# Graph attention on one core: owners' one-hot rows from squared distances on TensorE with one ScalarE pass, and the picked scores added in PSUM

## The chip, the cores and the metric

One Trainium2 chip, one of its NeuronCores. The metric is the device time of one execution in microseconds (us); a kernel is run several times and the median counts. Engines are called TensorE (PE in the profile, its weight loads PEld), VectorE (DVE), ScalarE (ACT), GpSimd (POOL) and SyncE (SP, which here only issues transfers).

## What is computed

Four graph layers after one another over 3125 nodes of 256 features and 100000 edges sorted by destination; each layer is added to `x`. Layers 0 (two convolutions) and 3 share this attention, here for one convolution with 4 heads:

```python
h = (x @ W).reshape(-1, H, C)
alpha_s = jnp.einsum('nhc,hc->nh', h, a_src)
alpha_d = jnp.einsum('nhc,hc->nh', h, a_dst)
e = jax.nn.leaky_relu(alpha_s[src] + alpha_d[dst], NEG_SLOPE)
m = jax.ops.segment_max(e, dst, num_segments=N)
ex = jnp.exp(e - m[dst])
s = jax.ops.segment_sum(ex, dst, num_segments=N)
alpha = ex / (s[dst] + 1e-16)
out = jax.ops.segment_sum(h[src] * alpha[:, :, None], dst, num_segments=N)
```

`alpha_s[src]` is one half of an edge's score (it comes with the gathered row), `alpha_d[dst]` the other (it is picked from a small table of the owners, the nodes that the edges are summed into). Layer 1 is a dot product attention, layer 2 a message sum; both keep their code.

## The kernel before

`sort_by_source` makes a second order of the edges; `units("d")` and `units("s")` cut each order into units, 128 edges that all belong to one group of 128 nodes, and store the lists and masks of the units in HBM. Then, layer by layer, `renew` projects the nodes and `attend` (lines 1354 to 1842) walks the edges. `attend` runs three times (tags 0a, 0b and none, here called stages 0a, 0b and 3); `attend_dot` and `aggregate_edges` are the stages of layers 1 and 2. Transfers that sort edges by source are spread over the stages (`moving`).

A stage of `attend` is 51 turns of 16 units (`STEP`). The order on each engine is written out by hand in its `step(t, sums, scores, spreads)`, which is called once per turn: turn t sums the units of turn t-1 (`sums`), computes the scores of the units of turn t, and prepares the owners' halves of turn t+1 (`spreads`). The lists `V`, `A` and `M` name the marks of VectorE, ScalarE and TensorE in this order, and `v.at(name, t)`, `s.at`, `m.at` are the counts that others wait for.

- GpSimd (1505) gathers a turn's 16 units, one indirect transfer of 128 rows each, with a memset of a buffer `pause` after each, three turns of buffers (`BUFS`) ahead. The slots of a quad (4 units) come free after its matmuls (`mm3`, `mm7`, `mm11`, `mm15`).
- TensorE: the transpose `scores` of the picked halves (1703) with 6 filling matmuls behind it (`keep_busy`, 104), then `reduce(0)`, `reduce(1)`, `reduce(2)`, each 4 fp32 matmuls one-hot x rows (1680), then 16 small matmuls `spread` (1692) that pick the owners' values with the one-hot rows `hot_r`, then `back_turned` (1723 and 1724, the exponentials back to columns), `reduce(3)`, 8 filling matmuls, and `joined` (1735), which turns the picked owners' values of the next turn round and adds their three bf16 parts.
- ScalarE: `extras` (1770) and `one_hot` (1759, 1763) for the quads' one-hots, `exp` (1796), `hot_rows` (1780, 1782), `alphas` (1810), `parts` (1816), `picked` (1823), `own` and `selfs` (1835, 1837). `hot_rows` makes the owners' one-hot rows of 8 units in two passes over 128 x 1024: an Abs of row minus partition number, and a Relu of one minus that. Its input `rows_r` is the row of the edges' owners, broadcast by SP to all 128 partitions (1465, 256 KB each).
- VectorE: `rescale`, `rows0` (1572), then a chain: `y` (1592, picked half plus own half), `leaky`, `withself` or `weigh`, the scans of the segment maximum, `under`, `shrink`, then `rows1`, `add0` to `add3` (1566), `rows2`, `add4` to `add7`, `rows3`, `add8` to `add15`, and `factor`.

```python
eng.wait_ge(vec, v.at(f"add{u - 4}", t) if u >= 4 else v.at(f"add{u + 12}", a))
```

ties matmul u to the addition that frees its PSUM bank: `mm4` waits for `add0`, and `add0` stands behind the whole chain of the scores and `rows1` on VectorE.

## Time and profile before

| | us |
|---|---|
| median of 3 timed runs | 7402.62 |
| lowest, highest | 7401.24, 7405.5 |
| span of the profiled execution, first to last instruction | 8931.6 |
| stage 0a of `attend` in it, from 997 to 2490 | about 1490 |

Only the span is known of the profiled execution, no time of its own beside it; it is 1529 us (20.7%) longer than the median of the timed runs. The profile page gives busy times over the span; over the whole of it GpSimd is busy 65%, TensorE 61%, VectorE 56%, ScalarE 43%, and the mean granted TensorE clock is 0.745. Times in the rows are in us from the start of the span unless marked ns. A matmul's end is modelled.

### The profile page before, as it was taken

How to read it: one execution, taken by the hardware profiler on the slowest of the kernel's cores; microseconds unless marked ns; L12 is line 12 of the kernel's file. 1: busy time of each engine (PE TensorE's matmuls, PEld its weight loads, DVE VectorE, ACT ScalarE, POOL GpSimd, SP SyncE). 2: the span in 40 equal slices, each digit the busy share in tenths (PEclk: the TensorE clock that was granted, in tenths of full speed). 3: DMA queues.
4: the chain of work that ended last, by engine and by line, in shares of the span. 5: the costliest groups of instructions: out<-in, count | busy, mean ns of one | idle time of the engine just before them, and what ended most of it. 6: DMA issues, size and time to landing. Idle time of an engine off the chain costs nothing. (4 is left out here: it accounts for less than half of the span.)

```text
span 8931.6 us, 130458 instructions
## 1 busy us (share of the span) xinstructions
PE 5412.5 (61%) x23088; PEld 4000.6 (45%) x23089; DVE 4963.7 (56%) x11653; ACT 3871.5 (43%) x9075; POOL 5847.5 (65%) x8186
## 2 busy tenths in 40 slices
PE   6442365666535656664676666658888754666665
PEld 5431244444424444443455555435555533444443
DVE  6444355555545555554677777744444445555556
ACT  2220255455424554552244444335555533454444
POOL 0555677777747777775467666657777765777774
PEclk9555677777767777776788988868888866777777
DMA  4112233333313333331466666423333323333332
GB/s 143 49 49 52 75 95 95 95 96 95 86 44 97 96 95 95 96 97 33 127 176 178 177 176 175 129 64 99 100 101 100 101 53 101 99 99 99 98 98 74
DMA packets 580940, 894.72 MB, mean 100 GB/s; under 512 B 307359, under 2 KB 357708, under 8 KB 580448
## 3 DMA queue, kind: packets, MB, share of 16 engines
q0 software_dynamic: 245984, 649.30, 26.7%
q1 hardware_dynamic: 334448, 218.84, 8.9%
q10 hardware_dynamic: 416, 25.60, 0.9%
q8 instruction: 27, 0.44, 0.0%
q14 instruction: 65, 0.53, 0.0%
HBM read 859.36 MB, written 59.47 MB: 103 GB/s over the span
## 5 line engine op out<-in xcount | busy, mean ns | idle before, releaser
L2002 POOL DMA_INDIRECT ad_ring<-tab_qv,ad_idx x808 | 770.7, 954 | 506.4 <-issue 217.6
L1515 POOL DMA_INDIRECT at_ring_0a<-tab_s,at_idx_0a x808 | 774.3, 958 | 430.9 <-PE at_po_0a L1680 219.2
L2396 POOL DMA_INDIRECT ae_ring<-tab_a,ae_idx x808 | 777.9, 963 | 423.0 <-PE ae_po L2553 233.7
L1515 POOL DMA_INDIRECT at_ring_0b<-tab_s,at_idx_0b x808 | 772.8, 956 | 426.7 <-PE at_po_0b L1680 213.2
L1515 POOL DMA_INDIRECT at_ring<-tab_s,at_idx x808 | 780.1, 965 | 377.6 <-PE at_po L1680 183.0
L1680 PE MATMUL at_po_0a<-at_rows_0a,at_hot_0a 128*128 128x264 f32 x1616 | 625.6, 560 | 520.8 <-ACT at_hr_0a L1780 199.8
L1680 PE MATMUL at_po_0b<-at_rows_0b,at_hot_0b 128*128 128x264 f32 x1616 | 624.3, 559 | 512.2 <-ACT at_hr_0b L1780 201.7
L1680 PE MATMUL at_po<-at_rows,at_hot 128*128 128x260 f32 x1616 | 614.5, 553 | 444.5 <-DVE acc L1566 179.0
L1680 PEld LDWEIGHTS at_po_0a<-at_rows_0a,at_hot_0a 128*128 128x128 f32 x1616 | 439.3, 282 | 670.8 <-DVE acc L1566 262.0
L1680 PEld LDWEIGHTS at_po_0b<-at_rows_0b,at_hot_0b 128*128 128x128 f32 x1616 | 438.5, 282 | 662.4 <-DVE acc L1566 264.4
L1680 PEld LDWEIGHTS at_po<-at_rows,at_hot 128*128 128x128 f32 x1616 | 435.9, 280 | 586.2 <-DVE acc L1566 225.4
L2182 PE MATMUL ad_pk<-node_a,ad_hr 128*128 x1616 | 485.0, 452 | 337.6 <-issue 193.1
L2546 PE MATMUL ae_pM<-ae_we,ae_featT 64*128 64x256 f32 x1616 | 508.0, 465 | 171.3 <-issue 114.5
L1566 DVE TENSOR_TENSOR acc<-acc,at_po_0a 128x264 f32 x808 | 314.0, 422 | 483.9 <-PE at_po_0a L1680 215.1
L1566 DVE TENSOR_TENSOR acc<-acc,at_po_0b 128x264 f32 x808 | 312.9, 422 | 481.5 <-PE at_po_0b L1680 212.2
L566 POOL DMA_INDIRECT recs_s<-rnk_recs_now,rnk_pos_now x294 | 288.8, 982 | 409.9 <-DVE rnk_both L466 176.2
L2182 PEld LDWEIGHTS ad_pk<-node_a,ad_hr 128*128 128x128 f32 x1616 | 350.6, 226 | 452.2 <-issue 396.8
L1566 DVE TENSOR_TENSOR acc<-acc,at_po 128x260 f32 x808 | 307.1, 418 | 437.7 <-DMA recs_s<-rnk_recs_now,rnk_pos_now 178.8
L2553 PE MATMUL ae_po<-ae_msg,ae_hot 128*128 128x256 f32 x1616 | 464.8, 439 | 98.1 <-issue 60.9
L2506 DVE TENSOR_TENSOR ae_pre<-ae_ring,ae_pM 128x1024 f32<-128x1024 f32 x202 | 246.6, 1221 | 493.4 <-PE ae_pM L2546 187.7
L2546 PEld LDWEIGHTS ae_pM<-ae_we,ae_featT 64*128 64x128 f32 x1616 | 351.2, 229 | 314.6 <-issue 178.7
L2353 DVE TENSOR_TENSOR acc<-acc,ae_po 128x256 f32 x808 | 291.5, 416 | 297.9 <-PE ae_po L2553 218.8
(508 smaller groups left out, 14085.4 us busy)
## 6 DMA issues: line engine op xcount, KB each, us to landing
at_rr_0a<-relrow_d SPq DMA_DIRECT2D x102, 256.0 KB
at_rr_0b<-relrow_d SPq DMA_DIRECT2D x102, 256.0 KB
ad_rr<-relrow_d SPq DMA_DIRECT2D x102, 256.0 KB
at_rr<-relrow_s SPq DMA_DIRECT2D x102, 256.0 KB
ae_feat<-attr_pad SPq DMA_DIRECT2D x808, 32.0 KB
rnk_lrow<-lorow_f SPq DMA_DIRECT2D x98, 256.0 KB
attr_pad<-in_edge_attr_dram ACTq DMA_DIRECT2D x1, 25000.0 KB, 79.1
at_ring_0a<-tab_s,at_idx_0a POOLq DMA_INDIRECT x808
```

The source lines that it names most:

```text
L566: eng.indirect_dma_start(out=order["s"]["recs"], out_offset=bass.IndirectOffsetOnAxis(ap=pos_now[:, t.slot, k:k + 1], axis=0), in_=recs_no ...
L1515: eng.indirect_dma_start(out=ring[:, t.slot * STEP + u, :], out_offset=None, in_=table, in_offset=bass.IndirectOffsetOnAxis(ap=idx[:, t.sl ...
L1566: v.did(f"add{u}", eng.tensor_tensor(to, to, po[:, u % 4:u % 4 + 1, 0:W], ALU.add))
L1680: m.did(f"mm{u}", eng.matmul(po[:, u % 4, 0:W], hot[:, q % 2, j, :], rows[:, q % 2, j, :, :].rearrange("p h f -> p (h f)"), start=True, st ...
L2002: eng.indirect_dma_start(out=ring[:, t.slot * STEP + u, :], out_offset=None, in_=table, in_offset=bass.IndirectOffsetOnAxis(ap=idx[:, t.sl ...
L2182: mm = eng.matmul(pk[:, p % 2, (u % 2) * D:(u % 2 + 1) * D], hot_r[:, u // HALF, (u % HALF) * P:(u % HALF + 1) * P], k_tab[:, bass.ds(gs[u ...
L2353: own(eng.tensor_tensor(to, to, out_ps(q, j), ALU.add), False)
L2396: eng.indirect_dma_start(out=ring[:, k, :], out_offset=None, in_=table, in_offset=bass.IndirectOffsetOnAxis(ap=idx[:, k:k + 1], axis=0))\
L2506: own(eng.tensor_tensor(pre[:, q % 2, :, :].rearrange("p (a u) f -> p a (u f)", a=2), ring[:, q * QUAD:(q + 1) * QUAD, :].rearrange("p (a ...
L2546: mm = eng.matmul(pM[:, j // 2, (j % 2) * D:(j % 2 + 1) * D], featT[:, q % 2, j, :], We[:, :], start=True, stop=True)
L2553: mm = eng.matmul(po[:, (q % 2) * 2 + j // 2, (j % 2) * D:(j % 2 + 1) * D], hot[:, q % 2, j, :], msg[:, q % 2, j, :], start=True, stop=True)
```

## The change

- `units` computes three rows per unit, `near`: the owner number (255 for edges that are no unit's own), and its square in two bf16 parts. Six VectorE instructions over 128 x 896 and three stores are added per call.
- In `attend`, SP loads `near` (3 partitions x 1024, 6 KB) in place of the broadcast rows. TensorE multiplies it with a constant `owner_rows` (2j, -1, -1) in four matmuls of 512 columns, `far0` to `far3`, into `far_bank` and `pb_bank`, which gives 2jr - r*r; ScalarE adds 1 - j*j as a bias and takes Relu, which is 1 where j equals r and 0 elsewhere: `owners0` to `owners3`, 128 x 512 each, from PSUM.
- `scores`, its 6 filling matmuls and VectorE's `y` are gone. The picked halves are added by one more matmul in `joined`'s accumulation, which now also waits for `picked`.
- `far0`, `far1` stand at the start of TensorE's turn, `far2`, `far3` between `reduce(0)` and `reduce(1)`; `owners0` and `owners1` open ScalarE's turn, `owners2` and `owners3` stand ahead of `one_hot(2)`.

```diff
+                    own(eng.scalar_tensor_tensor(out=own_f[:, :, :], in0=rel[:, :, :], scalar=FAR, in1=ok[:, :, :],
+                                                 op0=ALU.subtract, op1=ALU.mult))
+                    own(eng.tensor_scalar(own_f[:, :, :], own_f[:, :, :], FAR, None, ALU.add))
+                    own(eng.tensor_copy(near[:, 0, :, :], own_f[:, :, :]))
+                    own(eng.tensor_tensor(square[:, :, :], own_f[:, :, :], own_f[:, :, :], ALU.mult))
+                    own(eng.tensor_copy(near[:, 1, :, :], square[:, :, :]))
+                    own(eng.tensor_tensor(near[:, 2, :, :], square[:, :, :], near[:, 1, :, :], ALU.subtract))
...
+                    eng.wait_ge(chain, marks["near"])
+                    for part in range(3):
+                        eng.dma_start(od["near"][part, :, :].rearrange("(c p) e -> p c e", p=P), near[:, part, :, :])\
+                            .then_inc(saved, 16)
...
                     def feed_rows(t, h):
-                        eng.dma_start(rows_r[:, h, :], od["relrow"][bass.ds(t.n * STEP + h * HALF, HALF), :]
-                                      .rearrange("(o t) e -> o (t e)", o=1).to_broadcast([P, HALF * P])).then_inc(rows_in[h], 16)
+                        eng.dma_start(near[0:3, h, :], od["near"][:, bass.ds(t.n * STEP + h * HALF, HALF), :]
+                                      .rearrange("k t e -> k (t e)")).then_inc(rows_in[h], 16)
...
+                    eng.memset(near[:, :, :], 0.0).then_inc(blank, 1)
...
                         if scores:
-                            eng.wait_ge(mat, m.at("scores", t))
                             eng.wait_ge(act, s.at("own", a))
-                            v.did("y", eng.tensor_tensor(logits[:, 1, :], scores_in, logits[:, 0, :], ALU.add))
-                            done("y", t)
...
+                        def distances(p):
+                            h = p // 2
+                            if p % 2 == 0:
+                                eng.wait_ge(rows_in[h], t.n * 16 + 32)
+                            if p >= 2:
+                                eng.wait_ge(act, s.at(f"owners{p - 2}", t))
+                            m.did(f"far{p}", eng.matmul(far[p % 2], owner_rows[:, :],
+                                                        near[:, h, (p % 2) * QUAD * P:(p % 2 + 1) * QUAD * P],
+                                                        start=True, stop=True))
...
-                            m.did("scores", eng.transpose(scores_in, picked[:, :, :].rearrange("p h u -> p (h u)"), ident[:, :]))
-                            keep_busy(eng, spare_b, 6)
...
+                        distances(0)
+                        distances(1)
                         reduce(0)
+                        distances(2)
+                        distances(3)
                         reduce(1)
                         reduce(2)
...
-                                keep_busy(eng, spare, 8)
+                                keep_busy(eng, far_bank, 6)
                             eng.wait_ge(act, s.at("parts", t))
...
+                            eng.wait_ge(act, s.at("picked", t))
+                            eng.sem_inc(told, 1)
+                            m.did("joined", eng.matmul(joined[0:R, :], picked[:, :, :].rearrange("p h u -> p (h u)"),
+                                                       ident[:, :], start=False, stop=True, skip_group_check=True))
...
-                            s.did(f"far_r{h}", eng.activation(hot_r[:, h, :], rows_r[:, h, :], ACT.Abs, bias=minus_col[:, :]))
-                            done(f"far_r{h}", t)
-                            s.did(f"hot_r{h}", eng.activation(hot_r[:, h, :], hot_r[:, h, :], ACT.Relu, bias=ones[:, 0:1],
-                                                              scale=-1.0))
+                            eng.wait_ge(mat, m.at(f"far{p}", t))
+                            s.did(f"owners{p}", eng.activation(hot_r[:, p * QUAD * P:(p + 1) * QUAD * P], far[p % 2],
+                                                               ACT.Relu, bias=owner_bias[:, :]))
```

TensorE at the seam of two turns of stage 0a (`at_ta`, `at_tt`, `at_pe`, `at_po` are PSUM tiles of the scores, `joined`, the exponentials and the sums), before:

```order
L1680 MATMUL at_po_0a<-at_rows_0a,at_hot_0a 128x264
L107 MATMUL at_ta_0a<-ident 128x384 x8
L1733 REGISTER_ALU
L1735 MATMUL at_tt_0a<-ident,at_parts_0a 128x128 x3
L1699 REGISTER_ALU
L1701 REGISTER_ALU
L1703 MATMUL at_ta_0a<-ident,at_picked_0a 64x128
L107 MATMUL at_pb_0a<-ident 128x128 x6
```

And in the change:

```order
L108 MATMUL at_far_0a<-ident 128x512 x6
L1759 REGISTER_ALU
L1761 MATMUL at_tt_0a<-ident,at_parts_0a 128x128 x3
L1763 REGISTER_ALU
L1765 MATMUL at_tt_0a<-ident,at_picked_0a 64x128
L1712 REGISTER_ALU
L1715 MATMUL at_far_0a<-at_near_0a,owner_rows 128x512
L1715 MATMUL at_pb_0a<-at_near_0a,owner_rows 128x512
L1699 ISA
L1700 ISA
L1701 REGISTER_ALU
L1702 MATMUL at_po_0a<-at_rows_0a,at_hot_0a 128x264
```

The picked scores moved from a transpose of their own into `joined`'s tile; the two first distance matmuls stand where the six filling ones stood.

ScalarE from the start of a turn of stage 0a to the exponentials (`at_hr` is `hot_r`, `at_rows` the rows with the weights), before:

```order
L1770 ACTIVATE at_rows_0a<-at_al_0a 128x16x2
L1756 ISA
L1759 ACTIVATE at_hot_0a<-iota_row,at_nrel_0a 128x128 x4
L1746 REGISTER_ALU
L1763 ACTIVATE at_hot_0a<-at_hot_0a,ones 128x512
L1770 ACTIVATE at_rows_0a<-at_al_0a 128x16x2
L1795 ISA
L1796 ACTIVATE at_exp_0a<-at_less_0a 64x257
L1777 ISA
L1779 REGISTER_ALU
L1780 ACTIVATE at_hr_0a<-at_rr_0a,minus_col 128x1024
L1746 REGISTER_ALU
```

And in the change:

```order
L1799 ACTIVATE at_rows_0a<-at_al_0a 128x16x2
L1807 REGISTER_ALU
L1808 ACTIVATE at_hr_0a<-at_far_0a,owner_bias 128x512
L1807 REGISTER_ALU
L1808 ACTIVATE at_hr_0a<-at_pb_0a,owner_bias 128x512
L1785 REGISTER_ALU
L1788 ACTIVATE at_hot_0a<-iota_row,at_nrel_0a 128x128 x4
L1775 REGISTER_ALU
L1792 ACTIVATE at_hot_0a<-at_hot_0a,ones 128x512
L1799 ACTIVATE at_rows_0a<-at_al_0a 128x16x2
L1828 ISA
L1829 ACTIVATE at_exp_0a<-at_less_0a 64x257
```

The passes for the owners moved from behind the exponentials to ahead of the one-hots of quad 2.

## Rows read from the trace of the kernel before

**Rows 1.** Stage 0a: stretch; busy PE, PEld, DVE, ACT, POOL; clock, DMA share, GB/s.
```profile
970.00:2480.00 1510.00, 894.51 (x3711) 648.75 (x3711) 820.86 (x2004) 736.37 (x1727) 1064.35 (x1644) 0.73 0.35 94
```

**Rows 2.** Timeline, one turn of stage 0a: start, length, engine, line, tiles [idle before].
```profile
1702.46 0.48 DVE L1629 TENSOR_TENSOR_SCAN at_max_0a<-at_masks_0a,at_end_0a,at_full_0a 64x128 f32<-64x128 f32 x1
...
1705.36 5.65 PE L1680 MATMUL at_po_0a<-at_rows_0a,at_hot_0a 128*128 128x264 f32 x16 [4.77 <-ACT at_hr_0a L1780]
...
1713.99 0.33 PE L1724 MATMUL at_pe_0a<-ident,at_exp_0a 64*128 64x4 f32 x2
...
1714.25 2.05 PE L1680 MATMUL at_po_0a<-at_rows_0a,at_hot_0a 128*128 128x264 f32 x8
...
1717.57 0.28 ACT L1810 ACTIVATE at_al_0a<-at_pe_0a 128x128 f32<-128x128 f32 x1 [6.13 <-PE at_po_0a L1680]
...
1719.20 0.43 DVE L1566 TENSOR_TENSOR acc<-acc,at_po_0a 128x264 f32 x1 [6.81 <-DMA recs_s<-rnk_recs_now,rnk_pos_now]
...
1722.12 0.27 ACT L1835 ACTIVATE at_log_0a<-at_tt_0a 64x128 f32<-64x128 f32 x1 [1.78 <-DMA recs_s<-rnk_recs_now,rnk_pos_now]
...
1722.59 0.24 ACT L1770 ACTIVATE at_rows_0a<-at_al_0a 128x32 f32<-128x32 f32 x1
...
1723.99 1.21 DVE L1572 TENSOR_TENSOR at_rows_0a<-at_ring_0a,at_pe_0a 128x1024 f32<-128x1024 f32 x1
...
1725.43 3.88 PE L1680 MATMUL at_po_0a<-at_rows_0a,at_hot_0a 128*128 128x264 f32 x8 [5.78 <-DVE at_rows_0a L1572]
...
1727.15 0.28 DVE L1592 TENSOR_TENSOR at_log_0a<-at_ta_0a,at_log_0a 64x128 f32<-64x128 f32 x1 [1.95 <-PE at_po_0a L1680]
...
1731.17 0.48 DVE L1629 TENSOR_TENSOR_SCAN at_max_0a<-at_masks_0a,at_end_0a,at_full_0a 64x128 f32<-64x128 f32 x1
...
1731.29 0.24 ACT L1770 ACTIVATE at_rows_0a<-at_al_0a 128x32 f32<-128x32 f32 x1
...
1734.07 6.64 PE L1680 MATMUL at_po_0a<-at_rows_0a,at_hot_0a 128*128 128x264 f32 x16 [4.76 <-ACT at_hr_0a L1780]
```

**Rows 3.** Groups of instructions with forms, 1200 to 2300 us: count, busy us, mean ns, idle before.
```profile
L1515 POOL DMA_INDIRECT at_ring_0a<-tab_s,at_idx_0a x612 | 586.3, 958 | 315.3 <-PE at_po_0a L1680 184.1 <-issue 73.7 <-DMA recs_s<-rnk_recs_now,rnk_pos_now 36.4
...
L1519 POOL MEMSET at_pause_0a<- 128x256 f32 x611 | 199.7, 327 | 0.3
...
L1763 ACT ACTIVATE at_hot_0a<-at_hot_0a,ones 128x512 f32<-128x512 f32 x154 | 111.2, 722 | 5.0
L1782 ACT ACTIVATE at_hr_0a<-at_hr_0a,ones 128x1024 bf16<-128x1024 bf16 x76 | 87.2, 1148 | 2.5
L1780 ACT ACTIVATE at_hr_0a<-at_rr_0a,minus_col 128x1024 bf16<-128x1024 bf16 x76 | 86.1, 1133 | 0.0
...
L1816 ACT ACTIVATE at_parts_0a<-at_pb_0a 128x384 f32<-128x384 f32 x38 | 18.4, 485 | 0.0
...
L1823 ACT ACTIVATE at_picked_0a<-at_ring_0a 128x64 f32<-128x64 f32 x38 | 12.0, 316 | 0.0
...
L1703 PE MATMUL at_ta_0a<-ident,at_picked_0a 128*64 128x128 f32 x39 | 11.4, 292 | 0.0
...
L1592 DVE TENSOR_TENSOR at_log_0a<-at_ta_0a,at_log_0a 64x128 f32<-64x128 f32 x38 | 10.7, 283 | 85.2 <-PE at_po_0a L1680 62.5 <-ACT at_log_0a L1835 14.7 <-ACT at_rows_0a L1770 8.0
```

**Rows 4.** The addition `y` in stage 0a: count, min/median/max ns, first and last start.
```profile
L1592 DVE TENSOR_TENSOR at_log_0a<-at_ta_0a,at_log_0a x51: 282/283/284, 1024.3 to 2490.3; 64x128 f32<-64x128 f32 x51
```

**Rows 5.** Timeline of `units("s")`, VectorE and SP.
```profile
7424.58 0.63 DVE L729 CAST un_relb_s<-un_rel_s 128x896 bf16<-128x896 f32 x1
7425.23 0.40 SPq L824 DMA_DIRECT2D relrow_s<-un_relb_s  x1
...
7425.90 1.09 DVE L733 SCALAR_TENSOR_TENSOR un_ok_s<-un_rel_s,un_ok_s 128x896 f32<-128x896 f32 x1
```

**Rows 6.** Busy time by stretch, as Rows 1: under `reduce(3)` and under `reduce(0)`.
```profile
1714.20:1716.30 2.10, 2.10 (x11) 1.67 (x11) 0.00 (x0) 0.00 (x0) 1.80 (x3) 1.00 0.40 99
1725.40:1729.30 3.90, 3.87 (x8) 2.52 (x8) 1.75 (x7) 0.00 (x0) 2.61 (x5) 0.50 0.37 101
```

More of the change, by code:

```diff
@@ L1376, in attend @@
                 "add8", "add9", "add10", "add11", "add12", "add13", "add14", "add15", "factor"])
-        A = (["ext0", "away1", "hot1", "ext1", "away2", "hot2", "ext2", "exp", "far_r0", "hot_r0", "far_r1", "hot_r1",
+        A = (["owners0", "owners1", "ext0", "away1", "hot1", "ext1", "owners2", "owners3", "away2", "hot2", "ext2", "exp",
               "away3", "hot3", "ext3", "alphas", "parts", "picked", "away0", "hot0", "own"] + (["selfs"] if own_max else []))
-        M = ["scores", "mm0", "mm1", "mm2", "mm3", "mm4", "mm5", "mm6", "mm7", "mm8", "mm9", "mm10", "mm11",
-             "spread0", "spread1", "back_turned", "mm12", "mm13", "mm14", "mm15", "joined"]
+        M = ["far0", "far1", "mm0", "mm1", "mm2", "mm3", "far2", "far3", "mm4", "mm5", "mm6", "mm7", "mm8", "mm9", "mm10", "mm11",
+             "spread", "back_turned", "mm12", "mm13", "mm14", "mm15", "joined"]
         with ExitStack() as c:
@@ L1682, in reduce @@
                                                            start=True, stop=True))
[L1684 removed]
+                        def distances(p):
                             if not spreads:
[L1686 to L1691 removed]
+                                return m.skip(f"far{p}")
+                            h = p // 2
[6 more added lines that the diff above has]
+                                                        start=True, stop=True))
@@ L1692, in spread @@
+                        def spread(gs):
+                            if not spreads:
+                                return m.skip("spread")
+                            eng.wait_ge(act, s.at("owners3", t))
+                            for u in range(STEP):
                                 mm = eng.matmul(pb[:, u, :, :].rearrange("p k c -> p (k c)"),
-                                                hot_r[:, h, k * P:(k + 1) * P],
+                                                hot_r[:, u * P:(u + 1) * P],
@@ L1814, in step @@
                         if spreads:
-                            eng.wait_ge(mat, m.at("spread1", t))
+                            eng.wait_ge(mat, m.at("spread", t))
+                            if scores:
+                                eng.wait_ge(mat, m.at("joined", a))
                             s.did("parts", eng.activation(parts[:, :, :, :],
@@ L1836, in step @@
                             if own_max:
-                                s.did("selfs", eng.activation(logits[:, 2, :], joined[R:2 * R, :], ACT.Copy))
+                                s.did("selfs", eng.activation(logits[:, 1, :], joined[R:2 * R, :], ACT.Copy))
                         else:
```

94 lines of the change are left out of this document (45 added, 49 removed).

## The prediction

> **What bounds the kernel now.** I read the busy times of stage 0a first [rows 1]: in 1510 us GpSimd is busy 1064, TensorE 895, VectorE 821, ScalarE 736. No engine is full, so what sets a turn is either a chain of waits across engines or the pace of GpSimd. Then I read one turn in the timeline [rows 2]. The same scan starts at 1702.46 and 1731.17, so a turn is 28.7 us; three stages have 51 each, 153 turns.
>
> The chain goes round like this [rows 2]. VectorE multiplies the first rows at 1723.99 (1.21 us), then `y` starts at 1727.15 after 1.95 us of idle time, which is not a wait for data: 15 register loads (`groups`) stand between, and the two things that `y` waits for, the transpose and `own` (1722.12 plus 0.27), are long there. From `y` through the scans, `rows1` and `add0` VectorE needs 6.9 us until TensorE can start the eight matmul pairs of quads 1 and 2 at 1734.07. It has stood idle 4.8 us there, and `add0` is what it waits for in the code. Those sixteen instructions take 5.65 or 6.64 us, then come `spread`, `back_turned`, `reduce(3)`, the last additions, `factor`, `rescale` and the first rows of the next turn. So each instruction of VectorE between `y` and `add0` is on the ring; ScalarE's owner passes, SP's transfers and TensorE's `scores` are not, each ends before something later is due.
>
> GpSimd is the other limit: a gather takes 0.958 us, the memset behind it 0.327 [rows 3], and with the 0.16 us between them sixteen need 16 x 1.44 = 23.0 us. In the profile that leaves 5.7 us of each turn idle.
>
> The profiled execution spans 8931.6 us, the timed runs have a median of 7402.6, a factor of 0.829. The rows show one place where that time may lie: `back_turned` is issued at 1713.99 and ends by the model at 1714.3, but `alphas`, which waits for it alone, starts at 1717.57; the matmuls of `reduce(3)` are issued from 1714.25 on, but the first addition of one starts at 1719.20 [rows 2]. TensorE's marks arrive 3 to 5 us late there. If all stages shrink alike, a timed turn is 28.7 x 0.829 = 23.8 us, which is 0.8 us above GpSimd's 23.0. That nearness is the largest doubt of this prediction. Sums below are in us of the profiled execution and are carried over to the median unscaled, since instruction durations should be the same in both.
>
> **The change, part by part.**
>
> *VectorE's chain.* `y` goes: 283 ns [rows 4] and its own completion wait, 0.03 us between neighbours. 0.31 us per turn on the ring, x 153 = **-48 us**.
>
> *ScalarE.* Per turn 2 x (1.133 + 1.148) = 4.56 us of passes over 128 x 1024 go [rows 3]. Four Relus over 128 x 512 from PSUM come. The trace has none; bounds are the copy of 128 x 384 from PSUM at 0.485 us and the Relu of 128 x 512 from SBUF at 0.722 us [rows 3]. I take 0.65, being nearer to the size of the second: 2.6 us. ScalarE is relieved of 2.0 us per turn (1.7 to 2.6) at no gain, for its passes stood after `exp` and ahead of `one_hot(3)`, which waits for `mm7` anyway. What counts is where the new ones stand. `owners0` and `owners1` (1.3 us) now precede `extras(0)`, which ended at 1722.83, while the rows that `reduce(0)` also needs end at 1725.20: 2.4 us of cover. `owners2` and `owners3` wait for `far2` and `far3`, so `one_hot(2)` and `extras(2)` (ending at 1731.53) come later by 1.3 us and by the two matmuls; quad 2 is needed about 2.8 us behind 1734.07, so 5 us of cover. `exp` is pushed by about 1.2 us, and its reader `back_turned` comes 9 us later. If these covers went, the price is in the rivals.
>
> The Trainium skill, page "ScalarE: Activation LUTs", section "What ACT_TABLE_LOAD costs", gives about 280 ns plus 0.833 ns per element for an activation with a bias pointer, 707 ns for 512 columns as an estimate. That would be 2.8 us for the four, and since they lie off the ring the sum is the same.
>
> *TensorE.* Out: the transpose (0.29 us) and fillers of 6 x 128 columns. In: two distance matmuls of 512 columns in their place, about the same work, and two more between `reduce(0)` and `reduce(1)`, where it stood idle for 4.8 us [rows 2]; 1024 columns are 0.4 us at 2.4 GHz and 0.9 at 1.2. Zero on the ring. Fillers ahead of `joined` keep their 3072 columns. `joined` waits for `picked` too, which ScalarE does right behind `parts` (0.32 us), and has one fp32 matmul more (0.29 us, [rows 3]): up to 0.6 us later. `leaky` takes `own` at about 1727, 4.8 us after it is there, so this costs nothing while that holds.
>
> *SP and the DMA engines.* As many transfers per turn, 6 KB in place of 256 KB each. They are loaded two turns ahead and a matmul frees them earlier than the Relu did, so no queue waits longer. The DMA engines are 0.35 busy in the stage [rows 1]; taking 0.5 MB per turn from them frees nothing that is waited for. `feed_idx` waits for the previous `joined` in place of `scores`, issued back to back before.
>
> *`units`, twice.* Six VectorE instructions over 128 x 896 on its chain: three like the cast or scaling (0.63) and three with two inputs (1.09) [rows 5], 5.2 us, plus 6 x 0.03, about 5.4 us. After them come the evacuations that the stage's end waits for, so all of it shows: 2 x 5.4 = 10.8. The three stores add 3 x 0.40 us of issue on SP, in `units("s")` at its end, and some transfer time: 2 us, between 0 and 5. In `units("d")` they lie under the second list. **+13 us**.
>
> *Starts.* The memset of `near` is short of the 16 first gathers that the stage waits for, and the five tiny setup instructions run while VectorE waits for the inputs. Zero.
>
> Sum: -48 + 13 = **-35 us**, 8931.6 to 8897 in the profile and 7402.6 to **7368** in the timed runs. A measurement of this kernel can tell about 0.2%, 15 us, from no change.
>
> **The rivals.**
>
> *A, the forecast: the ring loses one instruction.* For it: of the 85.2 us that VectorE idles ahead of `y` in 38 turns only 14.7 are put down to `own` [rows 3]; the rest is the register loads. 7368.
>
> *B, GpSimd sets the timed turns.* If 23.0 us of gathers already decide there, a shorter chain only lengthens idle time elsewhere. For it: 23.8 against 23.0. Against it: GpSimd idles 5.7 us per turn in the profile. The change then also "does nothing" although it works. -0 + 13 = 7416, still within 0.2%.
>
> *C, `own` becomes the last to arrive (slower).* With TensorE's marks 3 to 5 us earlier in the timed runs, VectorE reaches `leaky` sooner, while `joined` still stands behind eight or six fillers and now also behind `picked` and a fourth product: +0.32 + 0.29, less the 0.31 of `y`, +0.3 us per turn, 46 us, with `units` 59: 7462. It decides from the point where `own`'s 4.8 us of cover fall under 0.6. For it: the turns in which `own` was already the releaser [rows 3]. ScalarE's new order would act at the same place with up to 1.3 us. Against it: the profile's cover.
>
> *D, TensorE's clock.* Under `reduce(3)` the granted clock is 1.00, which is 2.4 GHz, and eight instructions take 2.05 us; under `reduce(0)`, after TensorE has stood idle 5.8 us, it is 0.50, 1.2 GHz, and eight take 3.88 [rows 2, 6]. The sixteen of quads 1 and 2, after another idle 4.8 us, take 5.65 to 6.64 where 2 x 2.05 = 4.1 would do. `far2` and `far3` now lie in that gap. If they keep the clock up, a turn loses 1.5 to 2.5 us in the profile; in the timed runs GpSimd's 23.0 would stop it at 0.8 us per turn, -116, with `units` -103: 7300. Against it: 0.9 us of work in a gap of 4.8 is little.
>
> The Trainium skill, page "TensorE: Matmul & The Clock Gate", section "What's actually happening", says that half rate is the default and recent activity releases it; by that rule the filled gap speaks for D, and the trace agrees in that both slow stretches follow idle ones.
>
> **How the numbers follow.** A 0.42, B 0.26, C 0.22, D 0.10. Point 7368 from A. A's own range by the bounds (stores 0 to 5, 0.28 to 0.33 us per turn) is 7362 to 7375. The range reaches down to 7280, which takes in D, and up to 7460, the middle of C. Faster by over 0.2%: D and nearly all of A, 0.50. Within: most of B and the rest of A, 0.25. Slower: C and the part of B in which `units` costs over 15 us, 0.25.
>
> **What would show it.** Right: 153 turns of 28.4 us, `leaky` straight behind the register loads, four Relus of 0.59 to 0.72 us, VectorE busy about 33 us less in all (43 us of `y` less, 10 more in `units`). Against A: a turn unchanged in the profile with more idle time before `leaky` put down to `own` (C), more GpSimd share near 16 x 1.44 (B), or a granted clock well above 0.73 in the stages (D). The prediction is wrong if the time leaves the range, or if it moves in a stage other than these three and `units`.

## The result and the profile after

The changed kernel takes **7361.46 us** (median of 4 runs, 7357.06 to 7367.2), the kernel before in the same comparison 7404.06 (7401.24 to 7406.44): ratio 0.9943, 95% interval 0.9929 to 0.9957, 42.6 us faster. The forecast was 7368.

The profiled execution of before that the rows ahead come from was 20.7% longer than its timed runs; that of the changed kernel (span 7362.5) is as long as its own. The two can't be subtracted. So the kernel before was profiled again, unchanged (run e1_before below), with a span of 7395.2. "Before" means this second profile from here on, and the rows ahead are named by group.

From the two pages, engines' busy times and the queues of SyncE (q1) and of the instructions (q14), first before:

```profile
span 7395.2 us, 130458 instructions
PE 5003.2 (68%) x23088; PEld 3761.1 (51%) x23089; DVE 5017.3 (68%) x11653; ACT 3881.1 (52%) x9075; POOL 5854.0 (79%) x8186
...
q1 hardware_dynamic: 334448, 218.84, 10.9%
...
q14 instruction: 65, 0.53, 0.0%
```

and after:

```profile
span 7362.5 us, 129092 instructions
PE 5126.0 (70%) x22635; PEld 3674.3 (50%) x22636; DVE 4959.3 (67%) x11520; ACT 3550.9 (48%) x9075; POOL 5855.8 (80%) x8186
...
q1 hardware_dynamic: 297692, 141.87, 7.7%
...
q14 instruction: 140, 1.15, 0.0%
```

A queue's row gives its packets, the MB that they moved and their share of time. ScalarE is relieved of 330 us (2.2 us a turn), SyncE's queue moves 77 MB less, and the instruction queue moves 75 packets more, for which nothing in the change accounts.

Where the time went is read from one instruction that comes once a turn. `own` stands 51 times in each stage; the columns are its shortest, middle and longest duration in ns and its first and last start in us. Before:

```profile
L1835 ACT ACTIVATE at_log_0a<-at_tt_0a x51: 253/271/273, 847.4 to 2035.8; 64x128 f32<-64x128 f32 x51
L1835 ACT ACTIVATE at_log_0b<-at_tt_0b x51: 253/271/272, 2189.4 to 3378.1; 64x128 f32<-64x128 f32 x51
L1835 ACT ACTIVATE at_log<-at_tt x51: 253/255/273, 6165.7 to 7327.6; 64x128 f32<-64x128 f32 x51
```

After:

```profile
L1866 ACT ACTIVATE at_log_0a<-at_tt_0a x51: 252/253/270, 852.9 to 2004.4; 64x128 f32<-64x128 f32 x51
L1866 ACT ACTIVATE at_log_0b<-at_tt_0b x51: 252/253/270, 2163.9 to 3317.5; 64x128 f32<-64x128 f32 x51
L1866 ACT ACTIVATE at_log<-at_tt x51: 252/270/272, 6116.2 to 7295.3; 64x128 f32<-64x128 f32 x51
```

Fifty turns of 0a fall from 1188.4 us to 1151.5 (a turn from 23.77 to 23.03), those of 0b from 1188.7 to 1153.6 (23.77 to 23.07), and stage 3 **rises** from 1161.9 to 1179.1 (23.24 to 23.58). That is -36.9, -35.1, +17.2. Most of the rest is `units` (below). So there are three things to explain: why 0a and 0b gain more than twice the forecast 16 us each, why they stop at 23.0, and why stage 3 loses.

GpSimd's groups answer the second (why 23.0). Columns as in [rows 3]; first before, then after:

```profile
L1515 POOL DMA_INDIRECT at_ring<-tab_s,at_idx x808 | 780.5, 966 | 162.3 <-issue 98.7
L1515 POOL DMA_INDIRECT at_ring_0a<-tab_s,at_idx_0a x808 | 774.8, 959 | 159.6 <-issue 109.1
```

```profile
L1539 POOL DMA_INDIRECT at_ring<-tab_s,at_idx x808 | 782.6, 969 | 176.5 <-issue 97.3
...
L1539 POOL DMA_INDIRECT at_ring_0a<-tab_s,at_idx_0a x808 | 773.3, 957 | 139.1 <-issue 107.5
```

A gather costs the same as in [rows 3]. Its idle time in 0a falls to 139 us over 808 gathers, nearly all of it the 0.16 us from one instruction to the next: GpSimd has no free time left, and 16 x 1.44 = 23.0 us is the turn. Stage 3, whose gathers take 0.966 us, was at GpSimd's pace (23.2) before the change already. ScalarE's `picked`, which reads the gathered rows, shows the same from the other side: in 0a it waited for a gather in 9 of 51 turns before and in 50 of 51 after, in stage 3 in 42 of 51 before the change already.

TensorE's timeline of 0a changes too. Before, a turn from its `reduce(3)` (the first row of 128x264):

```profile
1508.47 2.05 PE L1680 MATMUL at_po_0a<-at_rows_0a,at_hot_0a 128*128 128x264 f32 x8
1510.35 1.46 PE L107 MATMUL at_ta_0a<-ident 128*128 128x384 bf16 x8
1511.65 0.83 PE L1735 MATMUL at_tt_0a<-ident,at_parts_0a 128*128 128x128 f32 x6
...
1514.15 2.04 PE L1680 MATMUL at_po_0a<-at_rows_0a,at_hot_0a 128*128 128x264 f32 x8 [1.23 <-DVE at_rows_0a L1572]
1522.86 6.50 PE L1680 MATMUL at_po_0a<-at_rows_0a,at_hot_0a 128*128 128x264 f32 x16 [6.66 <-ACT at_hr_0a L1780]
```

and after:

```profile
1499.40 0.40 PE L1765 MATMUL at_tt_0a<-ident,at_picked_0a 128*64 128x128 f32 x2 [1.21 <-ACT at_picked_0a L1854]
...
1503.20 3.60 PE L1702 MATMUL at_po_0a<-at_rows_0a,at_hot_0a 128*128 128x264 f32 x8 [2.63 <-ACT at_rows_0a L1799]
1506.63 0.38 PE L1715 MATMUL at_far_0a<-at_near_0a,owner_rows 128*128 128x512 bf16 x1
1506.85 0.38 PE L1715 MATMUL at_pb_0a<-at_near_0a,owner_rows 128*128 128x512 bf16 x1
1508.11 2.05 PE L1702 MATMUL at_po_0a<-at_rows_0a,at_hot_0a 128*128 128x264 f32 x8 [0.89 <-DVE acc L1591]
1510.60 2.05 PE L1702 MATMUL at_po_0a<-at_rows_0a,at_hot_0a 128*128 128x264 f32 x8 [0.44 <-ACT at_rows_0a L1799]
1513.08 2.10 PE L1724 MATMUL at_pb_0a<-b_tab,at_hr_0a 128*128 x16 [0.43 <-ACT at_rows_0a L1799]
```

Before, `reduce(0)` runs early and at full rate (2.04 us; its four fp32 matmuls stand as eight instructions, x8), TensorE then stands idle for 6.66 us until `add0` (the row names a ScalarE pass, but `mm4` waits for `add0` in the code), and the sixteen instructions of quads 1 and 2, which are on the ring, take 6.50. After, the same `reduce(0)` comes late and takes 3.60, off the ring, under VectorE's scans: between 2.04 and the 3.88 of [rows 2], which is half rate [rows 6]; the sixteen run at 2.05 us per eight and are through in 4.6. The granted clock says the same. The columns are those of [rows 1]; first before, `reduce(0)` and the first 4 us of the sixteen, then after, `reduce(0)` and quads 1 and 2:

```profile
1514.15:1516.19 2.04, 2.04 (x8) 1.43 (x8) 0.24 (x1) 1.20 (x4) 1.72 (x4) 1.00 0.41 95
1522.86:1527.00 4.14, 4.14 (x10) 3.21 (x11) 3.24 (x7) 3.55 (x4) 3.65 (x7) 0.50 0.54 144
```

```profile
1503.20:1506.80 3.60, 3.60 (x9) 2.69 (x10) 3.33 (x13) 1.89 (x6) 3.23 (x5) 0.56 0.39 101
1508.11:1512.65 4.54, 4.09 (x16) 2.87 (x16) 4.54 (x10) 4.47 (x14) 4.06 (x7) 1.00 0.43 114
```

Averaged over 45 turns of stage 0a, `reduce(0)` went from 2.08 to 3.71 us, the gap behind it from 6.47 to 1.05, and quads 1 and 2 from 6.31 to 4.86. That is 1.45 us a turn off the ring beside the 0.31 of `y`, where GpSimd's pace stops the turn after 0.74. Whether the turn needed those 1.45 us to come down to 23.0 is another question; the runs with the short pause below say that it didn't. The averages of this kind further down are over the same 45 turns.

### The profile page after: what moved, and what is told of

It reads as the page before. It is cut to its first block and busy times, and to the rows that moved or that the text cites. A ratio compares the mean times of both kernels' runs of the same rounds, so it can differ in the third digit from the quotient of the medians.

```text
span 7362.5 us, 129092 instructions
## 1 busy us (share of the span) xinstructions
PE 5126.0 (70%) x22635; PEld 3674.3 (50%) x22636; DVE 4959.3 (67%) x11520; ACT 3550.9 (48%) x9075; POOL 5855.8 (80%) x8186
## 3 DMA queue, kind: packets, MB, share of 16 engines
q14 instruction: 140, 1.15, 0.0%
## 5 line engine op out<-in xcount | busy, mean ns | idle before, releaser
L1702 PE MATMUL at_po<-at_rows,at_hot 128*128 128x260 f32 x1616 | 561.3, 514 | 306.8 <-DVE acc L1591 176.2
L1702 PE MATMUL at_po_0b<-at_rows_0b,at_hot_0b 128*128 128x264 f32 x1616 | 538.9, 490 | 188.1 <-DVE at_runf_0b L1632 90.2
L1702 PE MATMUL at_po_0a<-at_rows_0a,at_hot_0a 128*128 128x264 f32 x1616 | 537.5, 489 | 188.6 <-DVE at_runf_0a L1632 82.2
L2213 PE MATMUL ad_pk<-node_a,ad_hr 128*128 x1616 | 416.4, 403 | 216.6 <-DVE ad_prod L2110 188.0
L1702 PEld LDWEIGHTS at_po_0b<-at_rows_0b,at_hot_0b 128*128 128x128 f32 x1616 | 366.8, 238 | 344.8 <-DVE at_runf_0b L1632 153.4
L1702 PEld LDWEIGHTS at_po_0a<-at_rows_0a,at_hot_0a 128*128 128x128 f32 x1616 | 366.1, 238 | 345.3 <-DVE at_runf_0a L1632 149.5
L2577 PE MATMUL ae_pM<-ae_we,ae_featT 64*128 64x256 f32 x1616 | 450.8, 424 | 99.5 <-DVE ae_pre L2537 99.5
L2213 PEld LDWEIGHTS ad_pk<-node_a,ad_hr 128*128 128x128 f32 x1616 | 307.8, 198 | 319.5 <-issue 280.3
L2312 ACT ACTIVATE ad_hot<-iota_row,ad_nrel 128x128 f32<-128x128 f32 x808 | 257.4, 389 | 373.3 <-PE ad_po L2251 373.1
L2251 PE MATMUL ad_po<-ad_ring,ad_hot 128*128 128x264 f32 x1616 | 426.2, 404 | 11.0 <-DVE acc L2089 4.1
L1591 DVE TENSOR_TENSOR acc<-acc,at_po_0a 128x264 f32 x808 | 303.8, 416 | 166.8 <-PE at_po_0a L1702 163.7
```

Source lines behind the costliest of these rows:

```text
L1591: v.did(f"add{u}", eng.tensor_tensor(to, to, po[:, u % 4:u % 4 + 1, 0:W], ALU.add))
L1702: m.did(f"mm{u}", eng.matmul(po[:, u % 4, 0:W], hot[:, q % 2, j, :], rows[:, q % 2, j, :, :].rearrange("p h f -> p (h f)"), start=True, st ...
L2213: mm = eng.matmul(pk[:, p % 2, (u % 2) * D:(u % 2 + 1) * D], hot_r[:, u // HALF, (u % HALF) * P:(u % HALF + 1) * P], k_tab[:, bass.ds(gs[u ...
L2251: m.did(f"mm{u}", eng.matmul(po[:, u % 4, 0:W], hot[:, q % 2, j, :], ring[:, a.slot * STEP + u, D:D + W], start=True, stop=True))
L2312: ins = eng.activation(hot[:, q % 2, j, :], iota_row[:, :], ACT.Abs, bias=nrel[:, of.slot, k:k + 1])
L2577: mm = eng.matmul(pM[:, j // 2, (j % 2) * D:(j % 2 + 1) * D], featT[:, q % 2, j, :], We[:, :], start=True, stop=True)
```

## The experiments

Twelve runs were made beside that of the changed kernel. The first, of the kernel before, is a single execution; the others are medians. "Turn" is the time from the first to the last `own` of a stage, divided by 50, for stages 0a, 0b and 3.

| run | median us | before, same call | turn 0a | 0b | 3 |
|---|---|---|---|---|---|
| before, again | 7397.0 | 7403.0 | 23.77 | 23.77 | 23.24 |
| changed kernel | 7361.5 | 7404.1 | 23.03 | 23.07 | 23.58 |
| units only | 7418.8 | 7403.0 | 23.79 | 23.84 | 23.23 |
| join only | 7430.8 | 7403.0 | 23.29 | 24.34 | 23.94 |
| join only, loops moved | 7365.6 | 7401.5 | 23.41 | 23.44 | 23.27 |
| owners, y kept | 7350.4 | 7403.0 | 23.10 | 23.19 | 23.24 |
| changed, loop moved | 7348.1 | 7401.5 | 23.04 | 23.03 | 23.27 |
| the same, broadcast loads back | 7348.0 | 7404.1 | 23.03 | 23.03 | 23.28 |
| before, short memset | 7374.4 | 7401.5 | 23.78 | 23.60 | 23.01 |
| changed, loop moved, short memset | 7237.1 | 7401.5 | 22.69 | 22.30 | 22.50 |
| before, short memset, late reduce(0) | 7282.5 | 7404.1 | 23.13 | 22.91 | 22.64 |
| changed, all three | 7130.2 | 7404.1 | 21.92 | 21.84 | 21.52 |
| the last, more on ScalarE | 7130.0 | 7402.4 | 21.88 | 21.88 | 21.54 |

**e1_before**, the kernel before, unchanged.

> The kernel before, unchanged, for a profile whose span is near its timed runs (the one shown first spans 8931.6 us against a median of 7404). The changed kernel is 42.6 us faster and its turns in stages 0a and 0b take 23.03 and 23.07 us, sixteen times a gather and its pause; in stage 3 23.6 us. Theory T1 (a cross-engine ring still decides before, the change shortens it down to GpSimd's pace): a turn before takes 23.3 to 23.5 us in all three attend stages, GpSimd idles 0.3 to 0.4 us per turn in them. Theory T2 (before is at GpSimd's pace already): turns of 23.0 to 23.1 us in 0a and 0b before too, and the 42.6 us lie in stage 3 or outside of the attend stages. Theory T3 (the lighter transfers do it): gathers themselves or their landings take longer before, so GpSimd is equally busy but a gather costs more than 0.958 us.

Turns of 23.77, 23.77 and 23.24, a gather at 0.959. T3 has nothing to stand on here. T1 has the right cause in two stages of three, though the turn lies above its 23.3 to 23.5, and T2 holds in the third: there GpSimd's pace decided already, so a shorter ring can't gain.

**e4_units_only**, the six instructions and three stores alone.

```diff
+ own(eng.scalar_tensor_tensor(out=own_f, in0=rel, scalar=FAR, in1=ok, op0=subtract, op1=mult))
...
+ eng.dma_start(od["near"][part, :, :]..., near[:, part, :, :]).then_inc(saved, 16)
```

> The kernel before with only the six instructions over 128 x 896 and the three stores added in units; attend is as before. My term in the prediction was +13 us (10.8 of VectorE, 2 of stores, 0 to 5). If that holds: about 7404 + 13 = 7417 (7413 to 7422). If the list's other work hides it: 7404 within 5 us. T1 to T3 all expect the same here; it gives the price by which the gain of attend is larger than the 42.6 us seen.

+15.8 us (ratio 1.0023, 1.0014 to 1.0032). VectorE is busy 5028.5 against 5017.3, 11.2 more, where the term said 10.8. The rest, 4.6, is within the bound of 5 for the stores but isn't shown to be theirs: by the starts of `own`, 4 us come ahead of 0a, 10 between 0b and 3, and 3 inside 0b, which this edit doesn't touch.

**e5_join_only**, and with loops moved **e9_join_only_moved**. Both take `scores` and `y` out of the kernel before and add the picked halves in `joined`:

```diff
- m.did("scores", eng.transpose(scores_in, picked...))
+ eng.wait_ge(act, s.at("picked", t))
+ m.did("joined", eng.matmul(joined[0:R, :], picked..., start=False, stop=True))
...
- v.did("y", eng.tensor_tensor(logits[:, 1, :], scores_in, logits[:, 0, :], ALU.add))
```

> The kernel before with the picked halves added in joined's accumulation (scores and y gone, its 6 fillers kept at the start of the turn), broadcast rows and both passes over 128 x 1024 kept, nothing added in units. T1 with the y term of the prediction: a turn loses up to 0.31 us until GpSimd's 23.0 us stop it, 48 us: 7356 (7345 to 7370). If own arrives last because joined waits for picked (rival C's mechanism): no gain or slower, 7400 to 7450. T3: no gain, 7404, for the transfers are unchanged. T2: within 5 us of 7404 unless stage 3 gains.

Slower by 28 us (1.0034, 1.0022 to 1.0045), and it looked like rival C. But 0a gained and 0b, the same code, lost. In the waits of 2300 to 3200 (us in total, times, longest) and on its page stand two rows that before has not:

```profile
DVE acc L1582 <- issue: 41.8, 12, 3.9
```

```profile
q14 instruction: 214, 1.75, 0.1%
```

Twelve times in 900 us is once in three turns, once per lap of the loop. Each of stages 0b and 3 has fifteen such stops, 3.2 to 3.9 us each; the loop runs 16 laps and so jumps back 15 times. 149 packets more than before (214 against 65) came, five for each of the thirty jumps. The trace shows nothing else that is waited for there, which leaves the code as the suspect. The changed kernel has the same in stage 3 alone, fifteen stops of 5.1 to 6.1 us; in its timeline VectorE reaches `rescale` at the top of a lap:

```profile
6560.78 1.76 DVE L1591 TENSOR_TENSOR acc<-acc,at_po 128x260 f32 x4 [2.61 <-PE at_po L1702]
6562.46 0.22 DVE L1674 TENSOR_SCALAR at_pe<-at_pe,notfirst_s 128x4 f32<-128x4 f32 x1
6567.99 0.70 DVE L1607 TENSOR_TENSOR acc<-acc,at_pe 128x520 f32 x1 [5.31 <-issue]
```

Both kernels put empty instructions ahead of the stages (`pad=`), and the change shifted what stands behind them. So both were run with the loops moved:

```diff
-       columns=..., pad=29 if second else 0)        scatter=70, pad=14)
+       columns=..., pad=45 if second else 0)        scatter=70, pad=34)
```

(for the changed kernel, **e8_loop_moved**, only the second).

> The kernel before with only the picked halves moved into joined (scores and y gone), as in the earlier run, with 16 empty instructions more ahead of stage 0b and 20 ahead of stage 3 on VectorE. In the earlier run stage 0a gained 24 us (turn 23.77 to 23.29), while 0b and 3 lost 28 and 35 us with 3.9 us of idle time per three turns. If the place of the loops is all of that loss: 0b gains 24 us too, stage 3 is at 23.2 us, total 7403 - 48 = 7355 (7345 to 7365). If the joined accumulation costs where it is late: 7400 to 7431.

> The changed kernel with 20 more empty instructions on VectorE between two stages, ahead of stage 3, so that its loop of three turns starts 20 instructions later; no work is changed. In the changed kernel's stage 3 VectorE stands still for 5.3 us once in three turns with nothing to wait for, and the instruction queue moves 75 packets more than in the kernel before; before and the owners-only kernel show neither. If the place of the loop does it (code has to be brought again for each lap): the pauses and the 75 packets go, a turn of stage 3 falls from 23.58 to 23.2 us, the total to 7361 - 17 = 7344 (7335 to 7350). If the joined accumulation itself makes stage 3 slower: 7361, turn 23.6.

Both have the sign and the place that this cause asks for. Join only falls from 7430.8 to 7365.6 (just outside of the expected 7345 to 7365; 0a and 0b gain 18 and 17 us, not 24), the changed kernel from 7361.5 to 7348.1 (stage 3 from 1179.1 to 1163.7 for fifty turns), and both pages have the row of before again:

```profile
q14 instruction: 65, 0.53, 0.0%
```

The Trainium skill, page "Runtime: NRT & Kernel Launch", section "Instruction fetch mechanics", says that an engine other than TensorE holds 512 instructions in two blocks of 256, and that a taken branch to code outside of them has to wait for its block. By that a loop of VectorE is free only where it doesn't lie over three blocks. The trace agrees in kind: one stop of 3.2 to 6.1 us for each jump back, gone when the same loop starts 16 or 20 instructions later. What a jump moved, (1.15 - 0.53) MB / 15 = 41 KB, no sentence of the page explains.

Join only with moved loops is also the clean measure of the join and the missing `y`: the turns of 0a and 0b lose 0.36 and 0.33 us, stage 3 nothing, together -36 us (0.9956, 0.9943 to 0.9970).

**e6_owners_only**, the changed kernel with `scores` and `y` back. As the picked scores share a PSUM bank with `joined` here, `scores` also waits for `own` and `selfs`, which before it did not.

```diff
+ eng.wait_ge(act, s.at("selfs" if own_max else "own", a))
+ m.did("scores", eng.transpose(scores_in, picked...))
...
+ v.did("y", eng.tensor_tensor(logits[:, 1, :], scores_in, logits[:, 0, :], ALU.add))
```

> The changed kernel with scores and y put back (scores ahead of far0, without the six fillers behind it, y ahead of leaky), so only the owners' one-hots are changed, and units has its six instructions. By the prediction ScalarE's relief is worth nothing: the before time plus units' 13, 7417, and plus or minus 10 for the moved matmuls. If ScalarE's order or the 0.5 MB per turn of broadcast transfers carries the gain (T3): near 7361 to 7375. If the ring's y is all of it (T1 as predicted): 7405 to 7425.

-52.6 us (0.9928, 0.9914 to 0.9941): without the term that the forecast was made of, more than the whole gain, and faster than any of the three ranges expected. That killed the theory that `y` is all of it. It does not say which part of the owners' change acts, since the added wait holds TensorE back by some 4 us too:

```profile
1524.83 0.27 PE L1740 MATMUL at_tt_0a<-ident,at_picked_0a 128*64 128x128 f32 x1 [3.96 <-ACT at_log_0a L1882]
...
1526.93 3.44 PE L1706 MATMUL at_po_0a<-at_rows_0a,at_hot_0a 128*128 128x264 f32 x7 [1.36 <-DVE at_linef_0a L1634]
```

`reduce(0)` is late and slow here as well, and quads 1 and 2 take 4.80 us on average. What the two fast kernels share, besides the owners' change itself, is this lateness, and both are at GpSimd's pace.

**e13_wide_loads**, on the changed kernel with the moved loop.

```diff
+ eng.wait_ge(wide_in[h], t.n * 16 + 16)
+ eng.dma_start(rows_r[:, h, :], od["relrow"][...7 units...].to_broadcast([P, 7 * P])).then_inc(wide_in[h], 16)
```

> The changed kernel with the moved loop and, beside its small loads, the broadcast loads of the kernel before again (2 x 224 KB a turn into a tile that nothing reads). T3 (the lighter transfers bring the gain): back to 7385 to 7400. Otherwise: within 10 us of 7348, turns of 23.0 us in 0a and 0b, although the gathers land later and picked with them.

7348.0 against 7348.1, with the queue's bytes back at

```profile
q1 hardware_dynamic: 341756, 212.08, 10.8%
```

The traffic was worth nothing, in a kernel whose turn GpSimd sets and whose gathers take the same 0.956 us with it. T3 falls.

**e3_before_short_pause** and **e10_moved_short_pause**: GpSimd's memset halved, in the kernel before and in the changed one with the moved loop.

```diff
-            pause = sb(f"at_pause_{tag}", [P, 2, QUAD, 2 * P], F32, c)
+            pause = sb(f"at_pause_{tag}", [P, 2, QUAD, P], F32, c)
```

> The kernel before with the same shorter memset. Theory T1 (a ring through ScalarE's owner passes and VectorE decides in stages 0a and 0b, 23.77 us a turn; GpSimd's pace in stage 3, 23.24): 0a and 0b stay within 0.2 us of 23.77, stage 3 may fall to about 22.5: total 7403 less 10 to 50. If GpSimd's pace decided before too: as much gained as in the changed kernel with the short memset, 100 us or more.

> The changed kernel with the moved loop and GpSimd's memset behind each gather cut from 128 x 256 to 128 x 128, in the three attend stages. If GpSimd's pace sets the changed kernel's turn: 16 x about 0.13 us, 2 us, go from each turn until another engine stops it; TensorE is busy 0.70 and the ring of before ran at 23.8, so I expect 21.5 to 22.5 us a turn, total 7344 less 75 to 230 us. If another ring already decides at 23.0 us: 7344 within 10 us, with the new idle time on GpSimd put down to TensorE's matmuls. A third: gathers get slower by what the pause loses, 7344 again with a mean gather of 1.08 us.

The memset went from 328 ns to 221 and the pace to 16 x (0.957 + 0.221 + 0.16) = 21.4 us. Before gained 27 us: its 0a didn't move (23.78), so there the ring decides; stage 3 came down by 0.23 us, so its ring stood right behind GpSimd. The changed kernel gained 111, so GpSimd decided there, but it stopped at 22.3 to 22.7, at the upper end of the 21.5 to 22.5 expected. TensorE's timeline of 0a says why:

```profile
1504.29 2.04 PE L1702 MATMUL at_po_0a<-at_rows_0a,at_hot_0a 128*128 128x264 f32 x8 [1.63 <-ACT at_rows_0a L1799]
1506.17 0.38 PE L1715 MATMUL at_far_0a<-at_near_0a,owner_rows 128*128 128x512 bf16 x1
1506.39 0.38 PE L1715 MATMUL at_pb_0a<-at_near_0a,owner_rows 128*128 128x512 bf16 x1
1511.26 6.02 PE L1702 MATMUL at_po_0a<-at_rows_0a,at_hot_0a 128*128 128x264 f32 x16 [4.50 <-DVE acc L1591]
```

With gathers no longer late, `reduce(0)` is early again (2.14 us on average), and although `far2` and `far3` stand in the gap, the sixteen behind it take 6.0 to 6.9 us in this timeline, 6.20 on average.

This run also says what the changed kernel's lateness is worth. Here, **without** it, the ring takes 22.7, 22.3 and 22.5 us, which is under GpSimd's 23.0 already. So with the long memset GpSimd would have set the turn with an early `reduce(0)` as well: the late one came of waiting for the gathers and wasn't needed to reach 23.0. Stage 3 agrees: with the loop moved its quads 1 and 2 fall from 6.07 to 4.95 us, and the turn stays (23.24, 23.27).

What did shorten the ring is the difference of these two runs, in which `reduce(0)` is early in both. In 0a it is 1.1 us a turn: VectorE from the end of its first rows to `leaky` 2.33 to 1.87 us (`y` and what stands beside it), and three stretches of TensorE: quads 1 and 2 from 6.37 to 6.20, from their end to `reduce(3)` 2.59 to 2.42, `reduce(3)` 2.91 to 2.57. In 0b the three make 0.9 us together, in stage 3 only 0.15. The granted clock over 1000 to 1900 us is 0.80 in the first of these runs and 0.84 in the second, so less of TensorE's work is at half rate; what in the owners' change brings that, no run separates.

**e11_before_late** and **e12_moved_short_late** make `reduce(0)` late on purpose, in each of these two kernels.

```diff
- eng.wait_ge(vec, v.at(f"rows{q}", t))
+ eng.wait_ge(vec, v.at("turn1" if q == 0 and scores else f"rows{q}", t))
```

> The kernel before with the shorter memset and one wait changed: reduce(0) waits for turn1, the first small transpose of the score chain, in place of rows0, so it runs under the scans and TensorE stands idle before it, not between it and reduce(1). With the short memset alone the kernel took 7374.4, turns of 23.8, 23.6 and 23.0 us; there reduce(0) took 2.04 us at full clock, TensorE stood idle 6.7 us, and the sixteen instructions of quads 1 and 2, on the ring, took 6.4 to 6.8 us where 4.1 would do. Theory D2 (what made the changed kernel fast is that reduce(0) came late, so that the slow stretch of TensorE falls on work off the ring): quads 1 and 2 take 4.1 to 4.5 us, turns fall by 1.5 to 2.3 us to 21.4 to 22.2, total about 7374 - 75 to 110 in each of two stages: 7150 to 7260. Theory S (ScalarE's lighter passes made it fast): no gain or slower, 7374 to 7450, since one_hot(2) now starts later.

> The changed kernel with the moved loop, the short memset, and reduce(0) waiting for turn1. Without that wait it took 7237.1, turns of 22.7, 22.3 and 22.5 us, with TensorE idle for 5 us ahead of reduce(1) and its sixteen instructions at 6.0 to 6.9 us again. D2: the slow stretch moves off the ring, turns fall to GpSimd's pace, 16 x (0.957 + 0.221 + 0.16) = 21.4 us: total 7237 - 50 x (1.3 + 0.9 + 1.1), 7075 (7060 to 7130). S, or ScalarE becoming late for reduce(2): 7200 to 7280.

A wait more made both kernels faster: by 92 us (7374.4 to 7282.5) and by 107 (7237.1 to 7130.2). In 0a `reduce(0)` went from 2.04 to 3.48 us on average in the first and from 2.14 to 3.06 in the second, quads 1 and 2 from 6.37 to 5.42 and from 6.20 to 4.87. From the second's timeline:

```profile
1516.94 3.58 PE L1702 MATMUL at_po_0a<-at_rows_0a,at_hot_0a 128*128 128x264 f32 x8 [3.73 <-DVE at_runf_0a L1632]
1520.35 0.38 PE L1715 MATMUL at_far_0a<-at_near_0a,owner_rows 128*128 128x512 bf16 x1
1521.79 2.05 PE L1702 MATMUL at_po_0a<-at_rows_0a,at_hot_0a 128*128 128x264 f32 x8 [0.84 <-DVE acc L1591]
1524.28 2.05 PE L1702 MATMUL at_po_0a<-at_rows_0a,at_hot_0a 128*128 128x264 f32 x8 [0.44 <-DVE acc L1591]
```

D2 has the sign and the place: with the ring deciding, a late `reduce(0)` is worth 0.4 to 1.0 us a turn. Its size was too high in both: 7282.5 where 7150 to 7260 was expected, 7130.2 at the upper edge of 7060 to 7130. Not every turn gets the full rate, and the stretch from quads 1 and 2 to `reduce(3)` grew from 2.59 to 3.01 us in the first and from 2.42 to 3.03 in the second. In the kernel before, `spread` now waits for an owner pass in 21 of 39 turns, but for 9 us in all:

```profile
1510.57 2.19 PE L1692 MATMUL at_pb_0a<-b_tab,at_hr_0a 128*128 x16 [0.37 <-ACT at_hr_0a L1782]
```

**e14_more_scalar**: the fastest kernel with ScalarE's relief given back as two passes that nothing reads.

```diff
+ for k in range(2):
+     eng.activation(spent[:, k, :]..., iota_row..., ACT.Abs, bias=minus_col[:, :])
```

> The fastest kernel so far (the changed one with moved loop, short memset and late reduce(0), 7130.2 us) with ScalarE given back what the change took from it: two more passes over 128 x 1024, behind exp and ahead of one_hot(3), where the owner passes stood before, into a tile that nothing reads; 2.3 us a turn. The prediction took ScalarE's relief as worth nothing, since its passes end 2.8 us before they are needed. If that holds in this regime too: 7130 within 10. If the passes end on the ring once quads 1 and 2 run at full clock: up to 2.3 us x 153 turns more, and by the 152 us that this kernel leads the kernel before with the same two edits (7282.5, 53 of it the missing y and 16 against it units) I expect 60 to 120 us: 7190 to 7250.

```profile
L1832 ACT ACTIVATE at_spent_0a<-iota_row,minus_col 128x1024 bf16<-128x1024 f32 x102 | 110.8, 1133 | 0.0
```

2.27 us a turn more, and the time is the same (7130.0 against 7130.2). ScalarE's time as such is worth nothing even in the tightest kernel. The 7190 to 7250 that was thought likelier here is refuted; the prediction's view of ScalarE holds.

The kernel of e12_moved_short_late beats both: 7130.2 us, ratio 0.9635, 0.9621 to 0.9648.

## Why the prediction was right, and where its steps were not

- **The time** (7368, measured 7361.5) and the sign are right. That the size is right too is luck: two errors nearly cancel.
- **What bounds it.** "A timed turn is 28.7 x 0.829 = 23.8 us" is what the second profile shows for 0a and 0b (23.77). It is wrong for stage 3 (23.24), which GpSimd's pace set already: there rival B was true before the change. The lateness of TensorE's marks by 3 to 5 us [rows 2] was a trait of that long execution: in the second profile `back_turned` (1508.20) is followed by `alphas` at 1508.58.
- **y, -48.** The size per turn holds: 0.36 and 0.33 us by join only with moved loops, where 0.31 was said. The count was wrong, 102 turns and not 153, so -36.
- **ScalarE, no gain.** Holds for its time, by e14_more_scalar. The four Relus take 0.69 and 0.68 us, where 0.65 was taken.
- **TensorE, zero.** The step that failed. The working counted the columns put in and taken out and took the durations of all others as they were. But TensorE's stretches on the ring got shorter: by 0.7 us a turn in 0a and 0.9 in 0b with an early `reduce(0)` (short pause, before against changed). With `y`'s 0.35, which alone ends at 23.4, that takes the ring under GpSimd's 23.0. So the gain of 0a and 0b is the distance from 23.77 to GpSimd's pace, 0.74 and 0.70 us, and not the 0.31 of `y`.
- **`leaky`'s cover** of 4.8 us over `own`. It was 3.2 us in the second profile of before (`own` ends at 1512.79, `y` starts at 1515.95), and after the change it is gone: with GpSimd at its pace, `picked` waits for the gathers (waits of the changed kernel, 1000 to 1900):

```profile
ACT at_picked_0a L1854 <- DMA at_ring_0a<-tab_s,at_idx_0a: 222.0, 39, 6.1
...
DVE at_log_0a L1616 <- ACT at_log_0a L1866: 118.6, 39, 4.2
```

  `own` is last to arrive in each turn, as rival C had it. Behind `own` on ScalarE stand `owners0`, `owners1` and then `extras(0)`, for which `reduce(0)` waits; so `reduce(0)` slides under the scans, the slow stretch of TensorE falls on it, and quads 1 and 2 are 1.45 us faster. That makes slack and no time, since GpSimd sets the pace; for the same reason C did not cost what it said.
- **Rival D** named the resource, TensorE's clock, and that GpSimd would stop the turn at 0.8 (0.74 measured); the granted clock of 0a (1000 to 1900) went from 0.80 to 0.84. Its cause isn't what made quads 1 and 2 fast. It held that `far2` and `far3` keep the clock up in the gap. They lie in the gap of e10_moved_short_pause too, and the sixteen behind them take 6.0 to 6.9 us (6.20 on average against 6.37 without; whether that little is theirs isn't shown). The page "TensorE: Matmul & The Clock Gate" of the Trainium skill, section "What's actually happening", says that recent activity releases the full rate. The runs agree: 1.0 us of idle time ahead of quads 1 and 2 gave 4.9 us, and 4.5 to 5.0 us of it, behind `far2` and `far3`, gave 6.0 to 6.9.
- **Code loading** had no term at all. It cost some 15 us in stage 3 (1179.1 against 1163.7 with the loop moved), and it would have made the same change a loss in another layout (join only, +28 us where -36 was to be had).
- **units, +13.** Measured 15.8.
- **SP and the DMA engines, zero.** Holds: 0.46 MB a turn put back changes nothing.
- **VectorE busy 33 us less.** 58 less. The additions of stages 0a and 0b alone went from 317.9 and 318.5 us to 303.8 and 303.7, 28.9 us that had no term. With the broadcast loads back they are 304.2 and 304.5, so the lighter transfers aren't the reason; which it is stays open.

Put together: 0a and 0b -36.9 and -35.1, stage 3 +17.2, `units` +15.8 give -39.0; measured -42.6. The sum mixes stages of single profiles with medians and is good to some 10 us: the two profiled executions lie only 32.7 apart, and 5.9 us that came between stages 0a and 0b have no term. The forecast's -48 + 13 = -35 was near it by way of about 20 us too little in each of two stages and 33 too much in the third, which was to gain 16 and lost 17.

What stays open: why TensorE's stretches on the ring are shorter with the owners' change; and how the 152 us come about by which the changed kernel with both edits leads the kernel before with both. `y` explains about 53 of them (0.35 x 153), and 16 are lost in `units`. The averages of 0a say where the time is: quads 1 and 2 take 4.87 against 5.42 us, `reduce(3)` 2.46 against 2.75, VectorE up to `leaky` 1.87 against 2.33, while the stretch with `spread` is the same (3.03 and 3.01). So a `spread` that waits for an owner pass is not the difference.

## What to carry to other kernels

When TensorE has to stand idle somewhere in a turn, choose where: in these runs the work behind the idle time ran at half rate, so let that be work that nobody waits for, and keep the stretch on the ring directly behind other work. It pays only where that ring decides the turn (92 and 107 us here with the short memset, none seen where GpSimd set it: 23.24 and 23.27 in stage 3), so shorten the other engine's pace first and look again. Before crediting a shorter chain in every stage, look for the stages in which another engine's pace already sets the turn. And after any edit to an unrolled loop, compare the bytes of the instruction queue with the kernel before: a few packets more per lap mean that the loop now lies badly, which empty instructions ahead of it cured here.
